# Selective-scan kernel: scans that write to SBUF instead of back into their PSUM bank, and a share of C products for GpSimd that differs by position

## The reference

```
dt, Bp, Cp = split(h @ x_proj_w.T)          # h: the convolved, silu'd input
dt = softplus(dt @ dt_proj_w.T + dt_proj_b)
dA  = exp(dt[..., None] * A)                # (b, l, E, N)
dBu = (dt * h)[..., None] * Bp[:, :, None, :]
s_t = s_{t-1} * dA_t + dBu_t                # scan over l
y   = einsum('lben,bln->ble', states, Cp) + h * D
```

## Time and profile before

| | |
|---|---|
| median of 3 runs | 2318.58 us |
| the profiled execution's own time | 2318.14 us |
| its span | 2316.4 us |
| GpSimd (POOL) busy | 1966.7 us, 85% |
| VectorE (DVE) busy | 1929.6 us, 83% |
| TensorE (PE) busy | 1776.0 us, 77% |
| ScalarE (ACT) busy | 1472.4 us, 64% |
| mean granted TensorE clock | 0.907 of full |

### The profile page before, as it was taken

The page is one execution under the profiler, slowest core; times in us unless marked ns, Lnnn a source line. Parts: engine busy times, 40 slices in busy tenths (PEclk is TensorE's granted clock), DMA queues, the critical chain, the costliest instruction groups (busy, mean ns, idle before and its releaser), DMA issues.

```text
span 2316.4 us, 28669 instructions
## 1 busy us (share of the span) xinstructions
PE 1776.0 (77%) x8672; PEld 1316.5 (57%) x8672; DVE 1929.6 (83%) x2871; ACT 1472.4 (64%) x3939; POOL 1966.7 (85%) x1013
## 2 busy tenths in 40 slices
PE   6676777878778787777878778777878877787777
PEld 5364646556565655556555555655556565665553
DVE  2587888889888898888889888898988888898881
ACT  2466676666767667676766767666676757667550
POOL 0779989888898989989898998979889898988981
PEclk9788998989989999998999999899999989899778
DMA  5465204031220403113131311313122040302101
GB/s 184 156 121 127 76 24 132 24 136 37 78 87 29 131 25 124 50 65 96 33 123 33 119 55 34 122 38 119 37 94 80 20 136 22 135 23 79 51 14 37
DMA packets 69964, 179.82 MB, mean 78 GB/s; under 512 B 6577, under 2 KB 8241, under 8 KB 61618
## 3 DMA queue, kind: packets, MB, share of 16 engines
q1 hardware_dynamic: 66114, 170.65, 22.3%
q0 software_dynamic: 3696, 7.34, 2.0%
HBM read 169.05 MB, written 8.91 MB: 77 GB/s over the span
## 4 chain that ended last, share of the span: by engine, by line
POOL 38%; DVE 23%; PE 14%; ACT 11%; issue 11%; DMA 2%; DVEq 0%; POOLq 0%; ACTq 0%; SPq 0%
POOL ub L428 21%; POOL sc_p L448 11%; DVE decay L1079 9%; DVE bank_a L1126 4%; DVE sc_d L1089 4%; PE y_bank L780 3%; POOL u L408 3%; PE bank_a L825 3%; ACT decay L523 3%; DVE state L1079 2%; PE bank_c L899 2%; PE bank_a L857 2%; DMA ffn<-factors 2%; ACT L628 2%; ACT L523 2%
## 5 line engine op out<-in xcount | busy, mean ns | idle before, releaser
L523 ACT ACTIVATE decay<-dt,decay_rate 128x256 f32<-128x256 f32 (+1 forms) x2048 | 918.6, 469 | 486.1 <-DVE decay L1097 429.1
L428 POOL TENSOR_TENSOR ub<-u,b_all 128x2048 f32<-128x2048 f32 x256 | 1163.2, 4544 | 0.0
L1079 DVE TENSOR_TENSOR_SCAN decay<-decay,carry,ub 128x512 f32<-128x512 f32 x512 | 657.7, 1285 | 151.7 <-ACT decay L523 128.5
L448 POOL TENSOR_TENSOR sc_p<-state,c_all 128x1024 f32<-128x1024 f32 x256 | 603.0, 2356 | 203.8 <-DVE state L1079 203.7
L1079 DVE TENSOR_TENSOR_SCAN state<-decay,carry,ub 128x512 f32<-128x512 f32 x512 | 654.5, 1278 | 3.3 <-issue 1.3
L780 PE MATMUL y_bank<-ident,sc_d 128*128 128x128 f32 x2048 | 329.4, 292 | 234.3 <-DVE sc_d L1089 234.3
L780 PEld LDWEIGHTS y_bank<-ident,sc_d 128*128 128x128 f32 x2048 | 249.4, 149 | 359.0 <-DVE sc_d L1089 330.1
L780 PE MATMUL y_bank<-ident,sc_p 128*128 128x128 f32 x2048 | 323.9, 311 | 130.0 <-POOL sc_p L448 129.3
L780 PEld LDWEIGHTS y_bank<-ident,sc_p 128*128 128x128 f32 x2048 | 277.6, 162 | 165.4 <-POOL sc_p L448 149.9
L1089 DVE TENSOR_TENSOR sc_d<-decay,c_all 128x512 f32<-128x512 f32 x512 | 340.9, 666 | 0.0
L825 PE MATMUL bank_a<-hT,win_h 128*128 128x256 f32 x1024 | 265.4, 408 | 8.9 <-DVE hc L1137 4.9
(11 more groups left out here) (94 smaller groups left out, 1669.3 us busy)
## 6 DMA issues: line engine op xcount, KB each, us to landing
win_h<-win_m SPq DMA_DIRECT2D x128, 256.0 KB, 2.6
b_all<-bc_scratch SPq DMA_DIRECT2D x32, 1024.0 KB, 4.7
c_all<-bc_scratch SPq DMA_DIRECT2D x32, 1024.0 KB, 7.1
win_z<-win_m SPq DMA_DIRECT2D x128, 256.0 KB, 2.7
xa<-x SPq DMA_DIRECT2D x16, 512.0 KB, 6.0
xc<-x SPq DMA_DIRECT2D x16, 512.0 KB, 3.7
out<-xc SPq DMA_DIRECT2D x16, 512.0 KB, 6.8
ffn<-factors POOLq DMA_DIRECT2D x7, 1024.0 KB, 9.3
```

The costliest lines, as they stand in the source:

```text
L428: pool.tensor_tensor(ub[:, slot, :, :, :], u[:, 2 * q:2 * q + 2, :].unsqueeze(1).to_broadcast([P, QUAD, 2, ROWS]), b_all[:, n:n + QUAD, :] ...
L448: pool.tensor_tensor(sc_p[:, quad % 2, :, :, :], state[:, quad % 2, :, :, :], pair_c.to_broadcast([P, 2, 2, ROWS]), ALU.mult).then_inc(poo ...
L523: last = act.activation(decay[bank_of[unit]][:, j * ROWS + j:(j + 1) * ROWS], dt[:, pair % DT_PAIRS, j, j:], ACT.Exp, scale=decay_rate[:, ...
L1079: dve.tensor_tensor_scan(dst, bk[:, :], ub[:, quad % UB_RING, i, :, :].rearrange("p j r -> p (j r)"), carried_in[:, n, 2 * q:2 * q + 1], A ...
```

## The change

Every scan now writes to SBUF: to `state_d`, a ring of two, when VectorE multiplies it by C, and to `state_p`, a ring of eight, when GpSimd does; GpSimd's products are written in place there. The decay banks are only read by the scan, so the seam's zero stays, `free_bank` is gone, and the banks go round in order. How many of a quad's four units GpSimd multiplies is a table by position, `ON_POOL`, its last units: 2 at positions 0 to 3, 6, 9, 10 and 12; 3 at 4, 5, 7 and 8; 1 at 11, 13, 14 and 15. Their sum is 32 of 64 units, as before. VectorE's product of a unit comes one scan later for odd units. GpSimd's product now also waits for the carries of its quad (its output overwrites them). `sc_d` is a ring of three, `u` is a ring of three pairs made later, and some of ScalarE's, TensorE's and VectorE's side work is moved by a step or a few.

```diff
-D_RING = 4
+D_RING, D_STATES = 3, 2
+P_RING = 8
+U_PAIRS = 3
-ON_POOL = (1, 3)
+ON_POOL = (2, 2, 2, 2, 3, 3, 2, 3, 3, 2, 2, 1, 2, 1, 1, 1)
+def on_dve(unit):
+
+    quad, i = quad_of(unit)
+    return i < QUAD - ON_POOL[quad % QUADS]
...
             def multiply_c(quad):
...
-                wait(pool, turned_p, quad - 1)
                 pool.wait_ge(scanned, QUAD * (quad + 1))
-                pair_c = c_all[:, n:n + QUAD, :].rearrange("p (a i) r -> p a i r", i=2)[:, :, 1:2, :]
-                pool.tensor_tensor(sc_p[:, quad % 2, :, :, :], state[:, quad % 2, :, :, :],
-                                   pair_c.to_broadcast([P, 2, 2, ROWS]), ALU.mult).then_inc(pooled, 1)
+                pool.wait_ge(carried, carries_after(QUAD * quad + QUAD - 1))
+                k, slot = ON_POOL[g], first_slot(quad)
+                part = state_p[:, slot:slot + k, :, :]
+                pool.tensor_tensor(part, part, c_all[:, n + QUAD - k:n + QUAD, :].unsqueeze(2).to_broadcast([P, k, 2, ROWS]),
+                                   ALU.mult).then_inc(pooled, 1)
...
             def decays(unit):
...
+                if unit >= BANKS:
+                    act.wait_ge(scanned, unit - BANKS + 1)
+                    keep_carry(unit - BANKS)
...
             def scan(unit):
...
-                dst = bk[:, :]
...
+                if on_dve(unit):
+                    d = products_after(unit) - 1
+                    if d >= D_STATES:
+                        dve.wait_ge(multiplied, d - D_STATES + 1)
...
+                    dst = state_d[:, d % D_STATES, :, :]
...
             def multiply_c(unit):
...
-                dve.tensor_tensor(sc_d[:, i % D_RING, :, :], bk[:, :].rearrange("p (j r) -> p j r", j=2),
+                dve.tensor_tensor(sc_d[:, i % D_RING, :, :], state_d[:, i % D_STATES, :, :],
                                   c_all[:, n:n + 1, :].to_broadcast([P, 2, ROWS]), ALU.mult).then_inc(multiplied, 1)
-
-            def free_bank(unit):
-
-                if frees_before(unit) + BANKS >= UNITS * CHUNKS:
-                    return
-                dve.wait_ge(carried, carries_after(unit))
-                dve.memset(decay[bank_of[unit]][:, ROWS:ROWS + 1], 0.0).then_inc(bank_freed, 1)
...
                     scan(unit)
                     if unit:
-                        free_bank(unit - 2)
+                        multiply_c(unit - 1)
```

More of the change, by code:

```diff
@@ L69, in quad_of, with first_slot, turned_before @@
     return unit // QUAD, unit % QUAD
+def on_dve(unit):
+    quad, i = quad_of(unit)
+    return i < QUAD - ON_POOL[quad % QUADS]
 def products_after(unit):
-    return unit // 2 + 1
+    c, left = unit // UNITS, unit % UNITS + 1
+    return PRODUCTS * c + sum(on_dve(u) for u in range(left))
 def carries_after(unit):
[L79 to L98, removed]
+    return products_after(unit) + unit // QUAD + (not on_dve(unit))
+def first_slot(quad):
+    return sum(ON_POOL[:quad % QUADS]) % P_RING
+def turned_before(quad):
+    slots = set(range(first_slot(quad), first_slot(quad) + ON_POOL[quad % QUADS]))
+    before = quad - 1
+    while before >= 0 and slots.isdisjoint(range(first_slot(before), first_slot(before) + ON_POOL[before % QUADS])):
+        before -= 1
+    return before + 1
 def build(nc, x, win_m, xp_t, dt_t, wo_t, chan, cond_t, wmod, factors, bias, out):
@@ L457, in _ @@
             norm_before(0)
-            for q in range(PAIRS):
-                make_u(0, q)
+            make_u(0, 0)
             for quad in range(UB_RING - 1):
@@ L467, in one_round @@
                         make_ub(quad + UB_RING - 1)
-                    if la is not None and g == 1:
+                    if la is not None and g == 0:
                         norm_before(c + 1)
@@ L753, in _ @@
             last = CHUNKS - 1
+            for unit in range(UNITS * CHUNKS - BANKS, UNITS * CHUNKS):
+                keep_carry(unit)
             copy_y(PAIRS * CHUNKS - 1)
@@ L784, in turn_on_dve @@
             def turn_on_dve(unit):
[L786 to L788 removed]
+                if on_dve(unit):
+                    i = products_after(unit)
+                    pe.wait_ge(multiplied, i)
+                    turn_state(sc_d[:, (i - 1) % D_RING, :, :], False).then_inc(turned_d, 1)
             def turn_on_pool(quad):
                 pe.wait_ge(pooled, quad + 1)
[L793 to L794 removed]
+                k, slot = ON_POOL[quad % QUADS], first_slot(quad)
+                for i in range(k):
+                    last = turn_state(state_p[:, slot + i, :, :], i == k - 1 and quad % (N // QUAD) == N // QUAD - 1)
+                last.then_inc(turned_p, 1)
             def turn_states(step):
                 quad = step // 2
[L799 to L806, removed]
+                first = quad % (N // QUAD) == 0
+                if step % 2 and quad:
+                    turn_on_pool(quad - 1)
+                if step % 2 and first:
                     turn_skip(quad // (N // QUAD))
                     turn_on_dve(2 * step - 2)
+                if step % 2 or not first:
+                    if step:
+                        turn_on_dve(2 * step - 1)
                     turn_on_dve(2 * step)
@@ L1071, in scan @@
                     dve.wait_ge(ub_made, quad + 1)
-                dst = bk[:, :]
[L1073 to L1079, removed]
+                if on_dve(unit):
+                    d = products_after(unit) - 1
+                    if d >= D_STATES:
+                        dve.wait_ge(multiplied, d - D_STATES + 1)
+                        dve.wait_ge(carried, carries_after(max(v for v in range(unit) if products_after(v) == d + 1 - D_STATES and on_dve(v))))
+                    dst = state_d[:, d % D_STATES, :, :]
+                else:
+                    if i == QUAD - ON_POOL[quad % QUADS]:
+                        wait(dve, turned_p, turned_before(quad))
+                    dst = state_p[:, first_slot(quad) + i - QUAD + ON_POOL[quad % QUADS], :, :]
+                dve.tensor_tensor_scan(dst.rearrange("p j r -> p (j r)"), bk[:, :],
+                                       ub[:, quad % UB_RING, i, :, :].rearrange("p j r -> p (j r)"),
                                        carried_in[:, n, 2 * q:2 * q + 1], ALU.mult, ALU.add).then_inc(scanned, 1)
             def multiply_c(unit):
-                n, i, bk = unit % N, unit // 2, decay[bank_of[unit]]
+                if not on_dve(unit):
+                    return
+                n, i = unit % N, products_after(unit) - 1
                 if unit % UNITS < N:
```

98 lines of the change are left out of this document (42 added, 56 removed).

## The result

The changed kernel takes 2802.61 us, the median of four runs (2800.7 to 2804.32), against 2318.53 for the kernel before: a ratio of 1.209, 95% interval 1.207 to 1.211. It is 484 us slower. 2700 was forecast, with a range of 2430 to 3100, and 2600 to 2850 as the likeliest part of it.

The account below looks back on a forecast made before the run. POOL first, DVE close behind, were taken to bound the kernel; exclusion over SBUF reads raises a chunk from 137.1 to 161 us, 24 x 16 = 382 us on 2318.14, giving 2700 us, range 2430 to 3100.

Parts of the forecast that it names:

- exclusion decides: VectorE's 512 products with two SBUF inputs and GpSimd's SBUF instructions hold each other off to the end; 2600 to 2850, chance 0.5.
- three places in the clamping of `ga`: Trace evidence: L1190 took 2.86 us instead of 0.427; two POOL operations of 0.22 us took 0.64 and 0.66 under L1192.
- the sum: Time per chunk with exclusion, handed over at each instruction's end: 161 us against 137.1, 382 us more over the kernel.
- seven light ones: Quads with two units on POOL: period 9.3 us, or 8.3 where DVE got ahead; taken at 8.8, together 61.6 us.
- positions 4, 5, 7, 8: Quads with three units on POOL and side work on DVE: 9.4 + 9.4 + 10.6 + 9.4 = 38.8 us.
- position 6: Quad with two units on POOL and taps behind its last scan: 9.3 + 2.4 = 11.7 us.
- positions 11, 13, 14, 15: Quads with one unit on POOL and three products on DVE: 9.9 us each, four times 39.6 us.
- the carries: POOL's product waits for ScalarE's copy of last states: 0.2 us a quad, hidden while DVE is late.
- Rival (a): Exclusion, POOL keeps the port from its product to `ub`, DVE enters only behind `ub`: 3130 to 3180 us; chance 0.2.
- Rival (b): Exclusion that costs little, DVE waits for part of POOL's instruction or slips between: 2432 up to 2600 us; chance 0.14.
- Rival (c): No mutual exclusion in this form; part of POOL's 203.7 us wait goes: 2216 (half) or 2115 us (all); chance 0.13.
- Rival (d): As (c), but POOL's product waits for carries instead of scans, about 0.8 us a quad: 2318 us, no change; chance 0.03.

Follow-up runs that it names:

- the two exchanges of one operand: Product's operand exchanged: changed kernel reading the PSUM decay bank instead of `c_all`, 2293.39 us; kernel before reading `dtw` in SBUF instead of the PSUM bank, 2804.94 us.
- the uniform table: Changed kernel with two units of every quad on GpSimd: 2771.57 us; with GpSimd's product also in its own tile, not waiting for carries: 2674.74 us.
- the kernel with both products together: Changed kernel with two units of every quad on GpSimd and VectorE's two products side by side behind the quad's last scan: 2460.98 us, ratio 1.062.
- the kernel with the PSUM operand: Changed kernel with VectorE's C product reading the decay bank in PSUM in place of `c_all` in SBUF: 2293.39 us, ratio 0.990.

## Why the prediction was right, point by point

**What bounds it, and that exclusion decides: right.** Of the three places in the clamping of `ga` two told of the mechanism, those of L1192, and the two exchanges of one operand show it; L1190 reads a single SBUF operand, so that it was held is another case, which no run here varied. The open point, whether a product with two SBUF inputs waits to the end of a long GpSimd instruction, is settled: it does, up to 4.955 us. By the Trainium skill (SBUF — State Buffer, Who interferes with whom) the pair of ports that VectorE and GpSimd share is an exclusive lock. The trace agrees: the product that asked at 1375.12 ended 0.55 us behind the end of `ub`.

**The likeliest value was 103 us low (2700 against 2803).** A chunk is 167.0 us where the sum gave 161. The starts of GpSimd's products of positions 3 to 8 in one chunk:

```profile
1300.49 2.35 POOL L452 TENSOR_TENSOR state_p<-state_p,c_all 128x1024 f32<-128x1024 f32 x1 [1.60 <-ACT carry L506]
1312.12 4.05 POOL L452 TENSOR_TENSOR state_p<-state_p,c_all 128x1536 f32<-128x1536 f32 x1 [2.84 <-ACT carry L506]
1321.23 3.44 POOL L452 TENSOR_TENSOR state_p<-state_p,c_all 128x1536 f32<-128x1536 f32 x1
1329.86 2.35 POOL L452 TENSOR_TENSOR state_p<-state_p,c_all 128x1024 f32<-128x1024 f32 x1
1337.38 3.43 POOL L452 TENSOR_TENSOR state_p<-state_p,c_all 128x1536 f32<-128x1536 f32 x1
1348.65 3.45 POOL L452 TENSOR_TENSOR state_p<-state_p,c_all 128x1536 f32<-128x1536 f32 x1 [2.75 <-ACT carry L506]
```

From start to start, means of the third to the fifteenth chunk, set beside the terms of the sum:

| quads | measured, us | in the sum, us |
|---|---|---|
| seven light ones, with GpSimd's other work | 77.0 | 61.6 + 9.2 |
| positions 4, 5, 7, 8 | 40.8 | 38.8 |
| position 6 | 8.6 | 11.7 |
| positions 11, 13, 14, 15 | 40.8 | 39.6 |

The mis-sized term is the light two-unit quad: taken at 8.8 as the mean of 9.3 and 8.3 "where DVE has got ahead", measured 9.4 to 9.5 where no other work falls in. DVE, busy 95%, hardly gets ahead there. And *the carries*, taken as 0.2 us a quad and hidden, are in series: 0.4 us a quad, 97 us over the kernel, shown with the uniform table. That is about the size of the miss, and it isn't to be added to the light quads' 9.4, which contains it. Part of the closeness is luck: position 6 came out 3.1 us shorter than the sum had it, and in the chunk shown the four quads with three units took 11.6, 9.1, 7.5 and 11.3 us where 9.4 to 10.6 each was worked out, so only their sum is near.

**Rival (a), POOL keeps the port: wrong.** `ub` behind GpSimd's product takes 4.96 instead of 4.52 us where a product of VectorE was waiting: VectorE is let in between. **Rival (b), little cost:** wrong for this kernel at 2432 to 2600, but the kernel with both products together (2461) lies there, and the one with one such product a quad (2397) below it. A product took up to 4.80 and 4.25 us in them, so the exclusion is there too and costs less. **Rival (c), no exclusion:** wrong, and the 2293 us of the kernel with the PSUM operand is the nearest to what it would have given: closer to before than the 2115 to 2216 that I priced, and POOL still waited 178 us there for scans and carries. **Rival (d)** supposed no exclusion and falls with it; the wait for carries that it named is 0.4 us a quad where it was measured, not 0.8.

**The signs named:** product mean 2.12 (2 or more), maximum 4.96 (4.5 to 5), `ub` mean 4.74 (4.6 to 5), DVE 95%: as said. POOL's wait before its product is 490 us (350 or more), but the profile puts 487.9 of it down to the carries and 2.5 to the scans that I had named; only without the wait for the carries do the scans come last (316.9 us). The chunks are 167 us apart, not 161. GpSimd's two-unit product was not lengthened (2.356 as before), against what was said; what was lengthened instead is the seam's addition.

## What to carry to other kernels

Before moving an operand from PSUM to SBUF, count what the VectorE instruction that reads it then takes from SBUF: with two such inputs, and GpSimd busy on SBUF, the fp32 product here ran one at a time with GpSimd. The price was not a fixed one per instruction. One a quad, in a program with slack, cost 78 us for 256; two spread over the quad cost 487 for 512; the same 512 side by side behind the last scan cost 133 us above the same table without exclusion (443 us when spread). And a change of many parts can hide one that pays: undo or isolate its parts before it is kept or dropped.

## What was not expected of the hardware

The addition of four columns (0.21 us) grew to 0.54 us wherever a product of VectorE waited behind `ub`: the waiting engine got in at each end of an instruction of the other, in both directions (`ub` 4.52 to 4.96), and in the rows shown never had to let a second long one pass. In the kernel before with two SBUF inputs, three products took 5.6 to 6.2 us, all between 145 and 196 us, where GpSimd also issues its own DMAs:

```profile
145.62 6.14 DVE L1089 TENSOR_TENSOR sc_d<-dtw,c_all 128x512 f32<-128x512 f32 x1
```
```profile
145.38 1.28 POOL L455 DMA_DIRECT2D ffn<-factors  x1
146.21 4.99 POOL L428 TENSOR_TENSOR ub<-u,b_all 128x2048 f32<-128x2048 f32 x1
```

This product started by the profile 0.59 us ahead of `ub`, and still ended 0.56 us behind its end (151.76 against 151.20): here GpSimd was let in first, unlike in the relay. What the DMA issue has to do with it was not tried.
